# First attention of a small decoder on one core: normalisation in halves, a result's rest before maxima, copies behind exponentials

## The chip, the core and the metric

The kernel runs on one core of a Trainium2 chip. A core has five engines with an instruction stream each: TensorE (PE; its weight loads are shown apart as PEld), VectorE (DVE), ScalarE (ACT), GpSimd (POOL) and SyncE (SP). An engine takes its own stream in order, and the streams meet only at semaphores. The metric is device time in microseconds of one execution, smaller is better. The shown profile is one execution, with times counted from the first instruction of the program.

## The reference, cut to what matters

Two decoder layers over x of 16 sequences, 128 tokens and 256 features. The change touches the first sublayer alone, a 16-head attention with low-rank terms in its four weights:

```python
def _L0_attn_ref(x, Wq, bq, Bq, Aq, Wk, bk, Bk, Ak, Wv, bv, Bv, Av, Wo, bo, Bo, Ao):
    ...
    q = _split(lora_linear(x, Wq, bq, Bq, Aq))
    k = _split(lora_linear(x, Wk, bk, Bk, Ak))
    v = _split(lora_linear(x, Wv, bv, Bv, Av))
    scores = jnp.einsum('bhqd,bhkd->bhqk', q, k) * SCALE
    attn = jax.nn.softmax(scores, axis=-1)
    out = jnp.einsum('bhqk,bhkd->bhqd', attn, v)
    B, H, L, hd = out.shape
    out = out.transpose(0, 2, 1, 3).reshape(B, L, H * hd)
    return lora_linear(out, Wo, bo, Bo, Ao)
...
    x = x + _L0_attn_ref(_layernorm(x, axis=-1), ...)
    x = x + _L0_xattn_ref(ctx_2048, ctx_2048, _layernorm(x, axis=-1), L0_xattn_ssm_kernel, L0_xattn_D, 8)
    ...
```

## The kernel before, in words

The 16 sequences stay in on-chip memory as x, in four tiles of four. The attention (`stage_lora_attention`) has one loop of N = 64 steps n that each engine's block writes out in its own way: round g = n // 16 holds the four sequences of tile g, and step u = n % 16 of a round is one group of four heads of one sequence. The streams are written by hand; nothing schedules them. While round g computes its attention, the same loop prepares tile g + 1: its transposes, q, k and v.

What one group of heads n goes through, with the profile's lines: TensorE makes its scores in a bank (L343, for n + 4 and n + 5 in even steps); VectorE takes the negated maxima of each row (`row_max`, L589, for n + 3); ScalarE writes exponentials and row sums (`exps`, L520, for n + 2, four activations); VectorE inverts the sums (`inverse_sums`, L594, for n + 1); GpSimd multiplies the exponentials by them (`normalise`, L280, for n + 1); TensorE transposes the probabilities (`turn`, L353, for n); VectorE copies the transposed ones out (`keep_probT`, L599, for n); and TensorE multiplies them with the values (`weigh`, L365, for n - 1).

After four groups a sequence's result lies in one bank b_v. ScalarE takes its rounded half out (`keep_o`, L528), VectorE the rest (`o_rest`, L604), both in steps u = 1, 5, 9 and 13 for the sequence before; the next sequence's first `weigh` writes into the same bank and waits for that rest (`ot_lo`). `project` (L41 to L43) runs two steps later and `update` (L610) adds it to x.

The normalisation of a tile is VectorE's statistics (`vector_stats`, L112 to L119), a power on GpSimd (`pool_rstd`, L134), VectorE's application (`vector_apply`, L127), four transposes per half on TensorE (L139), and again a rounded half on ScalarE (`hi_chunk`, L146) and a rest on VectorE (`lo_chunk`, L150). Tiles 2 and 3 are normalised in rounds 0 and 1; the first tile of the next stage is in round 3. In round 2 VectorE adds a skip term instead (`add_skip`, L718), and GpSimd makes products for the next stage (L695) from step 31 on. In round 3 TensorE also runs convolutions for the next stage (L705 to L707), which ScalarE copies out (L713).

ScalarE copies q, k and v out of their banks in `keep_q` (L496, two activations), `keep_k` (L502) and `keep_v` (L512). TensorE makes these products at the end of steps 1, 5 (q), 3 with 7, 9 (k), 11, 13, 15 (v), each in bank b_p[0] or b_p[1], and waits for the copies before it uses the bank or the result again.

## Time and profile before

| what | value |
|---|---|
| time, median of 3 runs (all) | 1042.07 us (1040.94, 1042.07, 1046.86) |
| the profiled execution's own time | 1043.27 us |
| its span, first to last instruction | 1041.4 us |
| TensorE matmul busy | 968.2 us, 93% |
| VectorE, ScalarE, GpSimd busy | 61%, 47%, 23% |
| mean granted TensorE clock | 0.969 |
| first `turn` of the 64 steps, last one | 32.34 us, 195.84 us |

Busy shares are of the whole span, and the attention's 64 steps are under a sixth of it. A line of the timeline gives the start, the length, the engine, the line and the operation with its tiles; in brackets stands how long the engine was idle before it, and whose end released it. Matmuls overlap, so a matmul's busy time reaches over the start of the next one.

### The profile page before, as it was taken

The numbers are of one execution on the slowest core, as the hardware profiler recorded it, in microseconds if no ns is written. First come the engines' busy times: TensorE is split into PE (matmuls) and PEld (weight loads), VectorE is DVE, ScalarE is ACT, GpSimd is POOL, SyncE is SP. The second block draws the span as 40 slices with busy tenths as digits, with TensorE's granted clock in tenths as the row PEclk, the third lists the DMA queues.
The fourth block names the chain that finished last, engine by engine and source line by source line (L and its number), as shares of the span: only waits on it lengthen the run. The fifth ranks groups of instructions, "written<-read, shape, count | busy, mean of one in ns | idle before, by whom it ended". The sixth has DMA issues, their size and how long they took to land. (4 is left out here: it accounts for less than half of the span.)

```text
span 1041.4 us, 19631 instructions
## 1 busy us (share of the span) xinstructions
PE 968.2 (93%) x7397; PEld 827.0 (79%) x7397; DVE 639.3 (61%) x1399; ACT 484.8 (47%) x1611; POOL 238.3 (23%) x257
## 2 busy tenths in 40 slices
PE   7898989789989999999999999999999978899877
PEld 5676767689778888888888888888888857778757
DVE  5577777579757565654456644564464555777843
ACT  3577777533445454444444343444444433443421
POOL 3354677464002111111111111111111130110000
PEclk9899999989999999999999999999999998999969
DMA  7000000002240000000000000100000051000002
GB/s 298 2 2 2 2 2 2 25 1 82 82 162 2 1 1 1 2 1 2 1 1 2 1 1 2 41 1 1 1 1 1 1 177 83 2 1 1 3 1 81
DMA packets 10395, 27.85 MB, mean 27 GB/s; under 512 B 1792, under 2 KB 6944, under 8 KB 9664
## 3 DMA queue, kind: packets, MB, share of 16 engines
q1 hardware_dynamic: 9584, 26.41, 7.1%
q8 instruction: 60, 0.98, 0.4%
q10 hardware_dynamic: 720, 0.20, 0.1%
q14 instruction: 31, 0.25, 0.1%
HBM read 24.51 MB, written 2.10 MB: 26 GB/s over the span
## 5 line engine op out<-in xcount | busy, mean ns | idle before, releaser
L871 POOL TENSOR_TENSOR wa_prob<-wa_prob,wa_rsum 128x512 f32<-128x512 f32 x64 | 67.5, 1055 | 418.4 <-DVE wa_rsum L1409 418.4
L1213 ACT ACTIVATE wa_prob<-wa_prob,wa_negmax 128x128 f32<-128x128 f32 x256 | 99.8, 391 | 58.9 <-DVE wa_negmax L1398 58.7
L41 PE MATMUL bank<-norm_xT_hi,wide_hi 128*128 128x512 f32 x256 | 105.9, 414 | 2.2 <-DVE norm_xT_lo L150 1.4
L42 PE MATMUL bank<-norm_xT_lo,wide_hi 128*128 128x512 f32 x256 | 101.0, 395 | 0.0
L43 PE MATMUL bank<-norm_xT_hi,wide_lo 128*128 128x512 f32 x256 | 101.0, 395 | 0.0
L1465 DVE TENSOR_TENSOR wa_z_lo<-bank,wa_z_hi 128x512 fp32r<-128x512 f32 x64 | 44.3, 692 | 84.3 <-ACT wa_z_hi L1247 83.9
L520 ACT ACTIVATE v_prob<-bank,la_negmax 128x128 f32<-128x128 f32 x256 | 90.7, 386 | 1.2 <-DVE la_negmax L589 1.2
L1221 ACT COPY wa_q<-bank 128x512 f32<-128x512 f32 x64 | 37.6, 587 | 99.5 <-PE bank L43 99.5
L1228 ACT COPY wa_v<-bank 128x512 f32<-128x512 f32 x64 | 37.4, 585 | 97.5 <-PE bank L43 97.5
L280 POOL TENSOR_TENSOR v_prob<-v_prob,la_rsum 128x512 f32<-128x512 f32 x64 | 66.5, 1040 | 66.0 <-DVE la_rsum L594 65.9
L134 POOL TENSOR_TENSOR norm_rstd<-norm_rstd,minus_half 128x4 f32<-128x4 f32 x23 | 25.7, 1119 | 220.2 <-DVE norm_rstd L119 190.8
L41 PE MATMUL bank<-wide_hi,wa_z_hi 128*128 128x256 f32 x256 | 73.6, 287 | 1.7 <-DVE wa_z_lo L1465 1.4
L1404 DVE COPY wa_k<-bank 128x512 f32<-128x512 f32 x64 | 44.3, 692 | 50.3 <-PE bank L43 50.3
L1049 PEld LDWEIGHTS bank<-wa_probT,wa_v 128*128 128x128 f32 x512 | 65.4, 191 | 9.8 <-DVE wa_probT L1452 4.2
L43 PE MATMUL bank<-wide_hi,wa_z_lo 128*128 128x256 f32 x256 | 72.4, 283 | 0.0
L42 PE MATMUL bank<-wide_lo,wa_z_hi 128*128 128x256 f32 x256 | 72.3, 282 | 0.0
L1049 PE MATMUL bank<-wa_probT,wa_v 128*128 128x128 f32 x512 | 68.3, 276 | 1.9 <-DVE wa_probT L1452 1.9
L1452 DVE COPY wa_probT<-bank 128x512 f32<-128x512 f32 x64 | 44.1, 688 | 40.9 <-PE bank L1039 40.9
L998 PE MATMUL bank<-wa_k,wa_q 128*128 128x128 f32 x512 | 67.6, 275 | 0.0
L998 PEld LDWEIGHTS bank<-wa_k,wa_q 128*128 128x128 f32 x512 | 62.7, 192 | 0.4
L520 ACT ACTIVATION_READ_ACCUMULATOR v_prob<-bank,la_negmax 128x1 f32 x256 | 57.6, 225 | 0.0
L41 PEld LDWEIGHTS bank<-norm_xT_hi,wide_hi 128*128 128x128 f32 x256 | 48.2, 188 | 11.7 <-DVE norm_xT_lo L150 1.7
(273 smaller groups left out, 2473.0 us busy)
## 6 DMA issues: line engine op xcount, KB each, us to landing
wide_raw<-in_wide_w SPq DMA_DIRECT2D x16, 512.0 KB, 7.2
em_w<-in_em_w SPq DMA_DIRECT2D x1, 4096.0 KB, 15.0
x<-in_x SPq DMA_DIRECT2D x4, 512.0 KB, 4.9
lc_kt<-in_ctx_rev SPq DMA_DIRECT2D x1, 2048.0 KB, 10.3
lc_toep<-in_toeplitz SPq DMA_DIRECT2D x1, 2048.0 KB, 14.5
out_x<-x SPq DMA_DIRECT2D x8, 256.0 KB, 2.9
li_kt<-in_ctx_rev SPq DMA_DIRECT2D x1, 1536.0 KB, 7.3
w_or_y<-in_l_w SPq DMA_DIRECT2D x1, 1024.0 KB, 6.3
```

Source lines behind the costliest of these rows:

```text
L41: nc.tensor.matmul(out, a[0], b[0], start=start, stop=False, skip_group_check=True)
L42: nc.tensor.matmul(out, a[0], b[1], start=False, stop=False, skip_group_check=True)
L43: return nc.tensor.matmul(out, a[1], b[0], start=False, stop=stop, skip_group_check=True)
L280: nc.gpsimd.tensor_tensor(own, own, rsum[:, n % NS, :].unsqueeze(2).to_broadcast([P, 4, P]), ALU.mult)\
L520: last = nc.scalar.activation(prob[:, n % NP, s, :], b_s[n % RG][:, s * P:(s + 1) * P], ACT.Exp, bias=negmax[:, n % NS, s:s + 1], accum_ou ...
L871: nc.gpsimd.tensor_tensor(prob[:, s], prob[:, s], rsum[:, s, :].unsqueeze(2).to_broadcast([P, G, P]), ALU.mult).then_inc(prob_ok, 1)
L998: last = nc.tensor.matmul(b_s[s][:, t], q[:, s, t], k[:, s, t], start=True, stop=True)
L1049: last = nc.tensor.matmul(b_z[:, j * P:(j + 1) * P], v[:, g % 2, j, m * HD:(m + 1) * HD], probT[:, h_ % 2, j, :], start=True, stop=True)
L1213: last = nc.scalar.activation(prob[:, s, j, :], prob[:, s, j, :], ACT.Exp, bias=negmax[:, s, j:j + 1], scale=SCALE, accum_out=sums[:, s, j ...
L1404: nc.vector.tensor_copy(k[:, s, :], b_p[1][:, :]).then_inc(k_ok, 1)
L1452: nc.vector.tensor_copy(probT[:, t % 2], b_t[:, :].rearrange("p (j k) -> p j k", j=G))\
L1465: nc.vector.tensor_tensor(z[1][:, t % 2, :], b_z[:, :], z[0][:, t % 2, :].bitcast(F32), ALU.subtract).then_inc(z_lo, 1)
```

## The change

Three things move; no arithmetic changes. First, the statistics of a tile (four BN_STATS, then the aggregates) were all in step 3 of a round and the application in step 6. Now two BN_STATS are in step 3, two in step 5, the aggregates in step 6, GpSimd's power in step 6 instead of 3, and two applications each in steps 8 and 9. Second, `o_rest` comes before `row_max` (and `lo_chunk`) in its step. Third, `keep_q`, `keep_k` and the first `keep_v` of a tile come after the step's `exps` on ScalarE instead of before it (`extra_late`). Other stages still use the old functions.

```diff
--- before.py
+++ after.py
@@ -117,6 +117,31 @@
         chain.done(last)
         chain.close()
         nc.vector.tensor_scalar(self.rstd[:], self.meanvar[:, :, 1], EPS, None, ALU.add).then_inc(self.s_var, 1)
+
+    def vector_stats_half(self, dve, it, g, half):
+        for j in (2 * half, 2 * half + 1):
+            last = self.nc.vector.bn_stats(self.stats[:, j, :], self.pr.x[:, g * G + j, :])
+        if half == 1:
+            last.then_inc(self.s_chain, 1)
+
+    def vector_variance(self, dve, it):
+        nc = self.nc
+        dve.wait_ge(self.s_chain, 2 * (self.base + it) + 1)
+        nc.vector.memset(self.pr.wait_slot[:], 0.0)
+        for j in range(G):
+            last = nc.vector.bn_aggr(self.meanvar[:, j, :], self.stats[:, j, :])
+        last.then_inc(self.s_chain, 1)
+        dve.wait_ge(self.s_chain, 2 * (self.base + it) + 2)
+        nc.vector.tensor_scalar(self.rstd[:], self.meanvar[:, :, 1], EPS, None, ALU.add).then_inc(self.s_var, 1)
+
+    def vector_apply_half(self, dve, it, g, half):
+        if half == 0:
+            dve.wait_ge(self.s_pool, self.done(it))
+        for j in (2 * half, 2 * half + 1):
+            last = self.nc.vector.tensor_scalar(self.xn[:, j, :], self.pr.x[:, g * G + j, :], self.meanvar[:, j, 0:1],
+                                                self.rstd[:, j:j + 1], ALU.subtract, ALU.mult)
+        if half == 1:
+            last.then_inc(self.s_xn, 1)
 
     def vector_apply(self, dve, it, g=None):
         nc, x = self.nc, self.pr.x
@@ -228,8 +253,10 @@
 
 
 
-        STATS_AT, APPLY_AT, BIAS_AT = 3, 6, 10
+        STATS_AT, VAR_AT, POWER_AT, APPLY_AT, BIAS_AT = (3, 5), 6, 6, (8, 9), 10
         HI_AT, PROJECT_AT, ADD_AT = RG + 1, RG + 3, RG + 4
+
+        NORM_OF = {0: 2, 1: 3, NG - 1: NG}
 
         ORDER = (2, 0, 1, 3)
 
@@ -293,16 +320,14 @@
             for n in range(N - 1):
                 g, u = divmod(n, U)
                 normalise(n + 1)
-                if g + 2 < NG and u == STATS_AT:
-                    norm.pool_rstd(pool, g + 2)
+                if u == POWER_AT and g in NORM_OF:
+                    norm.pool_rstd(pool, NORM_OF[g])
                 if g + 1 < NG and BIAS_AT <= u < BIAS_AT + G:
                     add_bias(g + 1, u - BIAS_AT)
                 if FIRST <= n < FIRST + len(PIECES):
                     if n == FIRST:
                         pool.wait_ge(pr.conv_loaded, 16 * 4)
                     conv_piece(pr, *PIECES[n - FIRST]).then_inc(kk_first, 1)
-                if g == NG - 1 and u == STATS_AT:
-                    norm.pool_rstd(pool, NG)
 
         @block.tensor
         def _(pe):
@@ -536,7 +561,14 @@
                     return
                 if u == 1:
                     norm.hi_chunk(act, t, 1, b_p[0], xT[t % 2][0])
-                elif u == 2:
+                elif u == 11 and t + 1 < NG:
+                    norm.hi_chunk(act, t + 1, 0, b_p[0], xT[(t + 1) % 2][0])
+
+            def extra_late(g, u):
+                t = g + 1
+                if t == NG:
+                    return
+                if u == 2:
                     keep_q(t, 0, b_p[0])
                 elif u == 6:
                     keep_q(t, 1, b_p[1])
@@ -544,8 +576,6 @@
                     keep_k(t, 0, b_p[0])
                 elif u == 10:
                     keep_k(t, 1, b_p[0])
-                elif u == 11 and t + 1 < NG:
-                    norm.hi_chunk(act, t + 1, 0, b_p[0], xT[(t + 1) % 2][0])
                 elif u == 14:
                     keep_v(t, 0, b_p[1])
 
@@ -579,6 +609,8 @@
                     extra(g, u)
                 if n + 2 < N:
                     exps(n + 2)
+                if n < N:
+                    extra_late(g, u)
                 if N - U < n <= N:
                     keep_first_conv(n - (N - U) - 1)
 
@@ -610,19 +642,20 @@
                 nc.vector.tensor_tensor(x[:, b, :], b_p[1][:, 0:D], x[:, b, :], ALU.add).then_inc(x_ok, 1)
 
             def extra(g, u):
-                t = g + 1
-                if t + 1 < NG:
-                    if u == STATS_AT:
-                        dve.wait_ge(pr.x_loaded[t + 1], 16)
-                        norm.vector_stats(dve, t + 1)
-                    if u == APPLY_AT:
-                        norm.vector_apply(dve, t + 1)
-                if t == NG:
-                    if u == STATS_AT:
-                        dve.wait_ge(x_ok, G)
-                        norm.vector_stats(dve, NG)
-                    if u == APPLY_AT:
-                        norm.vector_apply(dve, NG)
+                it = NORM_OF.get(g)
+                if it is not None:
+                    own = it % NG
+                    if u == STATS_AT[0]:
+                        if it < NG:
+                            dve.wait_ge(pr.x_loaded[it], 16)
+                        else:
+                            dve.wait_ge(x_ok, G)
+                    if u in STATS_AT:
+                        norm.vector_stats_half(dve, it, own, STATS_AT.index(u))
+                    if u == VAR_AT:
+                        norm.vector_variance(dve, it)
+                    if u in APPLY_AT:
+                        norm.vector_apply_half(dve, it, own, APPLY_AT.index(u))
                 if g == 2:
                     if u == 0:
                         dve.wait_ge(pr.conv_loaded, 16 * 4)
@@ -658,15 +691,15 @@
                 g, u = divmod(n, U)
                 if n + 1 < N:
                     inverse_sums(n + 1)
+                b = batch_due(n, HI_AT)
+                if b is not None:
+                    o_rest(b)
                 if n + 3 < N:
                     row_max(n + 3)
                 if u == 1 and g + 1 < NG:
                     norm.lo_chunk(dve, g + 1, 1, b_p[0], *xT[(g + 1) % 2])
                 if u == 11 and g + 2 < NG:
                     norm.lo_chunk(dve, g + 2, 0, b_p[0], *xT[g % 2])
-                b = batch_due(n, HI_AT)
-                if b is not None:
-                    o_rest(b)
                 if n < N:
                     keep_probT(n)
                 b = batch_due(n, ADD_AT)
```

VectorE in steps 3 to 5 of a round; `norm_stats` are the statistics, `la_rsum` the inverted sums, `la_negmax` the maxima, `v_prob` the transposed probabilities. Before:

```order
L599 COPY v_prob<-bank 128x512
L112 BN_STATS norm_stats<-x 128x6 x4
L114 MEMSET wait_slot 1x1
L116 BN_AGGR norm_meanvar<-norm_stats 128x2 x4
L119 TENSOR_SCALAR norm_rstd<-norm_meanvar 128x4
L594 RECIPROCAL la_rsum<-la_sums 128x4
L589 TENSOR_REDUCE la_negmax<-bank 128x4
L599 COPY v_prob<-bank 128x512
L610 TENSOR_TENSOR x<-bank,x 128x256
L594 RECIPROCAL la_rsum<-la_sums 128x4
L589 TENSOR_REDUCE la_negmax<-bank 128x4
L604 TENSOR_TENSOR la_oT_lo<-bank,la_oT_hi 128x256
```

The same place of VectorE in the changed kernel:

```order
L631 COPY v_prob<-bank 128x512
L123 BN_STATS norm_stats<-x 128x6 x2
L626 RECIPROCAL la_rsum<-la_sums 128x4
L621 TENSOR_REDUCE la_negmax<-bank 128x4
L631 COPY v_prob<-bank 128x512
L642 TENSOR_TENSOR x<-bank,x 128x256
L626 RECIPROCAL la_rsum<-la_sums 128x4
L636 TENSOR_TENSOR la_oT_lo<-bank,la_oT_hi 128x256
L621 TENSOR_REDUCE la_negmax<-bank 128x4
L631 COPY v_prob<-bank 128x512
L123 BN_STATS norm_stats<-x 128x6 x2
```

Two BN_STATS instead of the whole group stand ahead of the first reciprocal, and in the second step the rest of the result stands ahead of the maxima.

ScalarE in steps 2 to 8 of a round; `la_q` and `la_k` are the copies, an `x4` of ACTIVATE is one group of heads. Before:

```order
L496 ACTIVATE la_q<-bank,la_q_bias,la_parity 128x512 x2
L520 ACTIVATE v_prob,la_sums<-bank,la_negmax 128x128 x12
L528 CAST la_oT_hi<-bank 128x256
L520 ACTIVATE v_prob,la_sums<-bank,la_negmax 128x128 x4
L496 ACTIVATE la_q<-bank,la_q_bias,la_parity 128x512 x2
L520 ACTIVATE v_prob,la_sums<-bank,la_negmax 128x128 x8
L502 ACTIVATE la_k<-bank,la_qk_bias 128x512
```

The same place of ScalarE in the changed kernel, from step 1 on:

```order
L545 ACTIVATE v_prob,la_sums<-bank,la_negmax 128x128 x8
L521 ACTIVATE la_q<-bank,la_q_bias,la_parity 128x512 x2
L545 ACTIVATE v_prob,la_sums<-bank,la_negmax 128x128 x8
L553 CAST la_oT_hi<-bank 128x256
L545 ACTIVATE v_prob,la_sums<-bank,la_negmax 128x128 x8
L521 ACTIVATE la_q<-bank,la_q_bias,la_parity 128x512 x2
```

Each copy has moved behind one group of exponentials.

## Rows read from the trace of the kernel before

**Rows 1.** Rounds 0, 1, 2: length; PE, PEld, DVE, ACT, POOL busy; granted clock; DMA.

```profile
32.34:75.83 43.49, 39.71 (x386) 29.88 (x386) 29.54 (x72) 30.17 (x142) 20.71 (x22) 0.90 0.01 2
...
75.83:117.21 41.38, 36.92 (x403) 28.11 (x401) 29.28 (x73) 30.64 (x144) 20.71 (x22) 1.00 0.01 2
...
117.21:158.33 41.12, 36.50 (x399) 27.62 (x397) 32.10 (x72) 29.99 (x143) 30.46 (x37) 1.00 0.01 2
```

**Rows 2.** Waits of TensorE's weighing, rounds 0 to 3: us, times, longest.

```profile
PE bank L365 <- DVE la_oT_lo L604: 1.2, 2, 0.7
...
PE bank L365 <- DVE la_oT_lo L604: 2.6, 3, 1.4
...
PE bank L365 <- DVE la_oT_lo L604: 4.6, 4, 1.4
...
PE bank L365 <- DVE la_oT_lo L604: 3.3, 4, 0.9
```

**Rows 3.** Waits of the transposes' weight loads, 28 to 204 us.

```profile
PEld bank L353 <- POOL v_prob L280: 8.1, 11, 2.1
```

**Rows 4.** Timeline, round 1, steps 2 to 5: start us, us, engine, line.

```profile
82.45 1.45 ACT L496 ACTIVATE la_q<-bank,la_q_bias,la_parity 128x512 f32<-128x512 f32 x2 [1.84 <-PE bank L43]
...
85.33 0.18 DVE L594 RECIPROCAL la_rsum<-la_sums 128x4 f32<-128x4 f32 x1 [1.75 <-ACT v_prob L520]
...
86.59 1.39 DVE L112 BATCH_NORM_STATS2 norm_stats<-x 128x6 f32<-128x256 f32 x4
...
86.79 0.42 PEld L353 LDWEIGHTS bank<-ident,v_prob 128*128 128x128 f32 x4 [0.39 <-POOL v_prob L280]
...
88.52 0.17 DVE L594 RECIPROCAL la_rsum<-la_sums 128x4 f32<-128x4 f32 x1
...
88.69 1.02 POOL L134 TENSOR_TENSOR norm_rstd<-norm_rstd,minus_half 128x4 f32<-128x4 f32 x1 [2.06 <-DVE norm_rstd L119]
...
90.77 0.66 PE L353 MATMUL bank<-ident,v_prob 128*128 128x128 f32 x4 [1.87 <-POOL v_prob L280]
```

**Rows 5.** Timeline, round 1, step 1.

```profile
78.05 0.41 ACT L528 CAST la_oT_hi<-bank 128x256 fp32r<-128x256 f32 x1
...
78.32 0.66 DVE L589 TENSOR_REDUCE la_negmax<-bank 128x4 f32<-128x512 f32 x1
...
79.22 0.69 DVE L150 TENSOR_TENSOR norm_xT_lo<-bank,norm_xT_hi 128x512 fp32r<-128x512 f32 x1 [0.24 <-ACT norm_xT_hi L146]
...
79.83 0.42 DVE L604 TENSOR_TENSOR la_oT_lo<-bank,la_oT_hi 128x256 fp32r<-128x256 f32 x1
...
80.39 0.43 PE L365 MATMUL bank<-v_prob 128*32 128x128 f32 x8 [1.39 <-DVE la_oT_lo L604]
```

**Rows 6.** Timeline, round 1, step 9.

```profile
99.92 0.37 ACT L528 CAST la_oT_hi<-bank 128x256 fp32r<-128x256 f32 x1
...
100.62 0.41 DVE L604 TENSOR_TENSOR la_oT_lo<-bank,la_oT_hi 128x256 fp32r<-128x256 f32 x1
...
101.19 0.43 PE L365 MATMUL bank<-v_prob 128*32 128x128 f32 x8 [0.74 <-DVE la_oT_lo L604]
```

**Rows 7.** Windows: step 5 of round 0, then step 5 of round 1.

```profile
47.94:51.66 3.72, 3.72 (x18) 2.55 (x19) 1.44 (x4) 0.04 (x1) 1.98 (x2) 0.54 0.00 0
...
90.77:92.97 2.20, 2.20 (x17) 1.62 (x18) 1.77 (x5) 0.04 (x1) 1.60 (x2) 1.00 0.00 0
```

**Rows 8.** Timeline, round 3, steps 9 and 10.

```profile
182.83 0.42 DVE L604 TENSOR_TENSOR la_oT_lo<-bank,la_oT_hi 128x256 fp32r<-128x256 f32 x1 [0.92 <-ACT la_oT_hi L528]
...
183.17 0.68 DVE L599 COPY v_prob<-bank 128x512 f32<-128x512 f32 x1
...
184.48 0.48 PEld L353 LDWEIGHTS bank<-ident,v_prob 128*128 128x128 f32 x4
```

**Rows 9.** One line's instructions, least, median and longest ns, rounds 0 to 3.

```profile
L718 DVE SCALAR_TENSOR_TENSOR lc_toep<-lc_anti,lc_skip,lc_toep x16: 341/574/1174, 118.9 to 157.6; 128x128 f32<-128x128 f32 x16
...
L127 DVE TENSOR_SCALAR norm_xn<-x,norm_meanvar,norm_rstd x12: 400/408/536, 53.1 to 176.2; 128x256 f32<-128x256 f32 x12
```

## Prediction

> **What bounds the kernel now.** I first read the windows over the rounds of the attention. In round 1 TensorE is busy for 36.92 of 41.38 us, VectorE for 29.28, ScalarE for 30.64 and GpSimd for 20.71; round 2 is alike, with VectorE at 32.10 of 41.12 [rows 1]. TensorE is the fullest engine by far, so its own idle time is what any reordering of the others can give back: about 4.5 us in each of the middle rounds, 11% of them. The reader is to see that no other engine is full: they matter by when they deliver, not by how much they do.
>
> Next I asked who TensorE waits for. Two things make up nearly all of it. `weigh` waits for `o_rest` 1.2 + 2.6 + 4.6 + 3.3 = 11.7 us, 13 times [rows 2]. And the weight loads of `turn` wait for `normalise` 8.1 us, 11 times, two of them over 2 us [rows 3]. Those last are mostly idle time of matmuls as well, but a short one hides under the last matmul's modelled end.
>
> Then the timeline says why. In round 1, ScalarE waits 1.84 us for the q product and copies it for 1.45 us, with the next exponentials behind it in its stream; VectorE's reciprocal for that group starts only at 85.33, 1.75 us idle; and `turn` of step 4 finds GpSimd 0.39 late at 86.79 [rows 4]. Right after, the statistics hold VectorE from 86.59 (four BN_STATS 1.39, then aggregates), so the reciprocal that `turn` of step 5 hangs on comes at 88.52; the power (1.02) stands ahead of its `normalise` on GpSimd; `turn` starts at 90.77 after 1.87 us of idle TensorE [rows 4]. In step 1, ScalarE had its half of the result at 78.05 + 0.41, but VectorE then did the maxima (0.66) and the xT rest, and only at 79.83 `o_rest`; `weigh` lost 1.39 us [rows 5].
>
> **The change, part by part.**
>
> *Statistics in halves, and copies behind the exponentials (one sum, since both make the same `turn` late).* The q copy's wait no longer stands before the exponentials of step 4: these need only their maxima and a free buffer, both there. So the reciprocal of `turn(4)` is limited by VectorE's own stream and the 0.39 goes. In step 3 two BN_STATS are left, 0.70 by half of 1.39. The reciprocal of `turn(5)` then stands behind 0.70 instead of 1.93 (86.59 to 88.52), and the power is not ahead of its product. TensorE's step 4 takes about 2.1 us (even steps without a wait: 2.20 in [rows 7]), more than reciprocal, `normalise` and their handovers together (86.79 to 88.9 against 0.17 + 1.04 + some 0.4), so `turn(5)` no longer waits. Of the 8.1 us in [rows 3] I leave 0.2 for each of five loads that have this gap with no wait at all, and 0.2 for the power, which in step 6 now stands ahead of the product for step 8: 8.1 - 1.0 - 0.2 = 6.9 us gained.
>
> Moved work costs: the second half of the statistics (0.70) is in step 5, aggregates and the added epsilon (some 0.5) in step 6, and two applications of 0.41 [rows 9] each in steps 8 and 9. They lie in VectorE's idle time (12.1 us in round 1, [rows 1]). Behind them stand one reciprocal each; for these the same 2.1 us of TensorE is the cover, and without it each would cost its own length, 0.5 to 0.8. The transposes of the new tile come in step 10, a step behind the last application, so nothing waits there. The waits inside the statistics are the old ones.
>
> The copies: q of step 2 now ends some 1.4 us behind its exponentials at worst. By this timeline the exponentials fit wholly into the 1.84 us in which ScalarE was idle, so q itself comes no later. The second k copy, wanted by the transposes at the end of step 10, has the least slack; I worked it through from step 1 with the rows' durations and find some 0.7 us left. Cost 0; without that cover up to 0.7 per round in three rounds, 2.1.
>
> *`o_rest` ahead of the maxima.* It cannot start before ScalarE's half. In step 9 of round 1 that half ends at 99.92 + 0.37 = 100.29, so `o_rest` could start near 100.33 instead of 100.62: `weigh`'s wait falls from 0.74 to 0.45 [rows 6]. So 0.45 is a floor: ScalarE's 0.37, VectorE's 0.41 and handovers, less the `turn` between. Thirteen waits at this floor are 5.9 us; 11.7 - 5.9 = 5.8 is the most that can go. Not all does. In step 1 of rounds 1 and 2 the next q product also needs the xT rest (0.69), which is pushed back behind `o_rest`, so of the gain of 0.94 there only about 0.4 stays, 1.1 lost on two. In round 3 `o_rest` already found VectorE idle, waiting 0.92 us for ScalarE [rows 8]; for three such steps, 1.0 us above the floor altogether, nothing changes. That leaves 5.8 - 1.1 - 1.0 = 3.7 us gained.
>
> *What comes back.* Steps 5 of rounds 0 and 1 have no `weigh` wait now because their `turn` is so late; once it is early they show the floor, 2 x 0.45 = +0.9. In round 3 the maxima (0.66) used to fill VectorE's wait for ScalarE; now they come after it, and push `keep_probT` from 183.17 to about 183.8. It ends at 184.5, and `turn` started at 184.48 [rows 8]: +0.2 on two steps, +0.4. In round 2 VectorE is fuller and `add_skip` takes 341 to 1174 ns [rows 9]; I allow +0.7 for round 2.
>
> *The clock.* Step 5 of round 0 ran at a granted clock of 0.54, 3.72 us against 2.20 for the same step of round 1 at 1.00 [rows 7]: the level of 1.2 GHz came right behind the step in which TensorE had idled. With that idle time gone I expect 2.4 GHz there: 1.5 us gained. The row that speaks against certainty: round 1 has the same idle time of 1.87 us [rows 4] and stayed at 1.00 [rows 1]. The Trainium skill ("TensorE: Matmul & The Clock Gate", What's actually happening) says that the half clock is the default, that activity releases it, and that the place of the switch depends on a phase the kernel does not set. By that rule the 1.5 may be absent or come back elsewhere, and the sum would be 1.5 less; the trace agrees, with its two equal gaps and one drop.
>
> *VectorE beside GpSimd.* `add_skip`, on two tensors, took from 341 to 1174 ns, while the twelve applications took 400 to 536 [rows 9]. I cost an application at its median of 0.41. The Trainium skill ("Perfetto Trace Analysis", Optimizing Scalar/DVE Operations) says that VectorE and GpSimd share a read port, which a two-port VectorE operation holds as an exclusive lock; it speaks against putting applications in two more steps beside GpSimd's products. By that rule an application could be as late as the longest `add_skip`, and the sum would be that of the second rival below.
>
> **Sum.** 6.9 + 3.7 + 1.5 - 0.9 - 0.4 - 0.7 = 10.1 us. From the profiled execution's own 1043.27 us that is 1033.2; from the median of 1042.07, 1.2 lower, 1032.0. Everything behind the attention is untouched. I take 1033.
>
> **Rivals.**
> *The clock does not repay (or dips elsewhere).* 10.1 - 1.5 = 8.6 gained: 1034 us (1034.7 from the profiled execution, 1033.5 from the median). For it: the two equal gaps above.
> *VectorE gives back half.* Its stream has 9 us of slack in a round 2 of 41 us [rows 1], 6.5 in one 2.3 shorter. If one application of each half waits for GpSimd's product and takes 1.17 like the longest `add_skip` instead of 0.54, a reciprocal or `o_rest` is 0.63 late at six places (3.8), and the second k copy behind them costs its 2.1: 10.1 - 5.9 = 4.2 gained, 1038.5 us, as the middle between the two starting points. For it: the 1174 ns. Against it: applications have been at 536 ns at the most.
> *It doesn't do what it says.* The wait for a result's rest is really ScalarE's, and the two long waits of `turn` (2.1 each, [rows 3]) come back at `weigh`. Then 10.1 - 3.7 - 4.2 = 2.2 is gained: 1040.5 us. For it: three places of round 3. Against it: [rows 5, 6] have VectorE busy with other work while the half lay ready.
> *Slower: VectorE stands before ScalarE's half with the maxima behind it.* There are 14 steps with both. A maximum can be late by 0.41 + 0.66 = 1.07 and more where ScalarE is late (0.92 idle before `o_rest`, [rows 8]). If all 14 reach the exponentials and so `turn`, that costs 15.0, and a TensorE that idles this often does not get its clock back either: 1042.07 + 15.0 - 8.6 = 1048.5 us. It takes the whole gain from 8.6 / 14 = 0.6 per step on. For it: an in-order stream behind a wait. Against it: maxima run one step ahead of their exponentials (n + 3 against n + 2), a step being 2.1 us or more.
>
> **Numbers.** The forecast 0.50, clock 0.17, half given back 0.18, nothing moved 0.10, slower 0.05. The range reaches from 1028 (neither the 1.1 and 1.0 lost nor the 0.4 and 0.7 given back, 13.3 gained from the median, and 0.8 for the runs' own spread) to 1040, which takes in the half given back and most of the third rival. A measurement of this kernel can tell about 0.5%, 5.2 us, from no change. The first two cases are faster, half of the third is too, a little of the others: faster 0.77, within 0.5% 0.18, slower 0.05.
>
> **What would show it.** In the changed kernel's profile: rounds 0 to 3 shorter by about 4.7, 2.9, 2.3 and 0.2 us (the terms above by their rounds); no wait of `turn` for `normalise` over 0.5 us after the first step; the waits of `weigh` for `o_rest` near 0.45 each, some 15 of them and 7 to 8 us in all; no idle ScalarE before L521 with exponentials behind it; the clock at 1.00 from step 2 on. Wrong would be: reciprocals late behind applications in steps 8 and 9; `row_max` late with ScalarE idle for it; TensorE waiting for a q or k copy; or the rounds shorter and the time behind 204 us longer.

## The result, and the profile after

The changed kernel takes 1031.84 us in the median of 5 runs (1030.38 to 1032.77), the kernel before beside it 1042.72 (5 runs, 1040.94 to 1046.86): a ratio of 0.9892, with an interval from 0.9872 to 0.9911. That is 10.9 us, inside the range of the prediction and 1.2 from its 1033. The profiled execution is one of the 1030.38 us, with a span of 1028.6 at a mean granted clock of 0.972.

The windows over the four rounds and over all of them; columns as in [rows 1]:

```profile
30.27:68.48 38.21, 36.81 (x386) 28.25 (x386) 29.32 (x72) 29.70 (x142) 21.07 (x22) 0.96 0.01 2
68.48:107.22 38.74, 36.65 (x403) 28.30 (x401) 29.19 (x72) 30.07 (x144) 21.26 (x23) 1.00 0.01 2
107.22:145.43 38.21, 36.11 (x399) 27.78 (x398) 30.81 (x73) 29.58 (x143) 30.02 (x37) 1.00 0.01 2
145.43:182.63 37.20, 34.08 (x381) 27.63 (x380) 25.54 (x64) 26.56 (x131) 26.32 (x31) 1.00 0.01 2
30.27:182.63 152.36, 143.66 (x1560) 111.95 (x1561) 114.86 (x280) 115.92 (x560) 98.68 (x110) 0.99 0.01 2
```

Busy times hardly moved: VectorE 29.19 us in round 1 after 29.28, ScalarE 30.07 after 30.64 [rows 1]. Round 1 is 2.64 us shorter, nearly all of it because TensorE idles 2.1 us in it instead of 4.5. The rounds are 5.29, 2.64, 2.91 and 0.31 us shorter, where 4.7, 2.9, 2.3 and 0.2 were forecast. They are 11.2 us together. The other 1.7 of the 12.9 between the two profiled executions lie where nothing was changed: the first round starts at 30.27 instead of 32.34, and what follows the rounds takes 0.4 longer. Over the fourteen kernels of this study that start lies anywhere from 30.27 to 32.54, and what follows the rounds takes 843.1 to 846.0 us. So I compare kernels by the length of the four rounds ("the loop"), less steps 0 to 2 of round 0, whose clock depends on what came before them: 154.46 us before, 144.31 after. A step runs from the first weight load of one `turn` to that of the next.

Whom TensorE waits for, 28 to 204 us: us, times, longest.

```profile
PE bank L390 <- DVE la_oT_lo L636: 7.2, 13, 0.9
...
PEld bank L378 <- issue: 6.8, 21, 2.8
...
PE bank L378 <- POOL v_prob L307: 2.6, 1, 2.6
```

The row of [rows 3], weight loads of `turn` (now L378) waiting for `normalise`, is not there any more. The one wait of `turn` for `normalise` that is left is that of the attention's very first group, 2.6 us, which the kernel before has too. `weigh` (L390) still waits for `o_rest` 13 times; nine of these are 0.45 or 0.46, one 0.48, three 0.88.

The timeline of round 1, steps 2 to 5, the place of [rows 4]:

```profile
74.49 1.49 ACT L521 ACTIVATE la_q<-bank,la_q_bias,la_parity 128x512 f32<-128x512 f32 x2
...
77.57 0.74 DVE L123 BATCH_NORM_STATS2 norm_stats<-x 128x6 f32<-128x256 f32 x2
78.23 0.16 DVE L626 RECIPROCAL la_rsum<-la_sums 128x4 f32<-128x4 f32 x1
78.47 1.04 POOL L307 TENSOR_TENSOR v_prob<-v_prob,la_rsum 128x512 f32<-128x512 f32 x1 [1.64 <-DVE la_rsum L626]
...
80.69 0.42 PEld L378 LDWEIGHTS bank<-ident,v_prob 128*128 128x128 f32 x4 [0.20 <-issue]
80.83 0.37 ACT L553 CAST la_oT_hi<-bank 128x256 fp32r<-128x256 f32 x1 [2.06 <-PE bank L390]
81.24 0.42 DVE L636 TENSOR_TENSOR la_oT_lo<-bank,la_oT_hi 128x256 fp32r<-128x256 f32 x1 [0.77 <-ACT la_oT_hi L553]
81.81 0.43 PE L390 MATMUL bank<-v_prob 128*32 128x128 f32 x8 [0.46 <-DVE la_oT_lo L636]
```

The q copy waits for nothing. Two BN_STATS (0.74) stand ahead of the reciprocal where four and the aggregates stood, and GpSimd multiplies at once: its product ends at 79.51, more than a microsecond before `turn` of step 5 loads. The price stands in the last three rows: ScalarE now sits idle until TensorE has finished a matmul, VectorE until ScalarE has taken the half, and TensorE in turn sits idle 0.46 us while the half (0.37) and the rest (0.42) are copied. With ScalarE and VectorE both idle ahead of their copies, no other order of VectorE can lower this floor.

### The profile page after: what moved, and what is told of

It is laid out like the page before. It is cut to its first block and busy times, and to the rows that moved or that the text cites. A ratio compares the mean times of both kernels' runs of the same rounds, so it can differ in the third digit from the quotient of the medians.

```text
span 1028.6 us, 19631 instructions
## 1 busy us (share of the span) xinstructions
PE 962.5 (94%) x7397; PEld 824.2 (80%) x7397; DVE 637.1 (62%) x1399; ACT 482.9 (47%) x1611; POOL 238.2 (23%) x257
```

## The experiments

Theory: the gain is the sum of TensorE's waits that the three parts take away, each part's own as the prediction's sum has them, and the clock of one step. Rivals: parts take away each other's waits; the clock is chance; what still stands is set by TensorE's own order. Edits are against the changed kernel. All times are medians beside the kernel before on the same chip (1041.85, 17 runs, for the three with one part and `whole_power6`; 1042.37, 11 runs, for the three with one part undone and `rest_late_round3`; 1042.24, 11 runs, for `half_before_conv`, `product_first`, `product_lo_first` and `all_first`), but for the changed kernel, whose 1031.84 stands beside 1042.72.

### One part alone

`stats_only`, the statistics in halves without the two other parts:

```diff
+                    extra_late(g, u)
                 if n + 2 < N:
                     exps(n + 2)
-                if n < N:
-                    extra_late(g, u)
...
-                b = batch_due(n, HI_AT)
-                if b is not None:
-                    o_rest(b)
                 if n + 3 < N:
                     row_max(n + 3)
...
+                b = batch_due(n, HI_AT)
+                if b is not None:
+                    o_rest(b)
```

> The kernel before with only the statistics and normalisation in halves (copies still ahead of the exponentials, the rest of a result behind the maxima). My theory: TensorE's transposes of step 5 in rounds 0 and 1 lose their 2 us waits, and the slow clock of that step in round 0 goes too, but the wait for the rest of a result shows itself there with over 1 us, as in round 2. About 3.5 us faster than before, 1039 us; rounds 0 and 1 shorter by 2 to 3 and by 1, rounds 2 and 3 by 0.3 or less. Rival (the gain is mostly the start ahead of the loop and its clock, by luck): rounds 1 to 3 as before, and no difference from before beyond 1 us.

`rest_only`, `o_rest` ahead of `row_max` alone; the first hunk above and this one:

```diff
-        STATS_AT, VAR_AT, POWER_AT, APPLY_AT, BIAS_AT = (3, 5), 6, 6, (8, 9), 10
+        STATS_AT, POWER_AT, APPLY_AT, BIAS_AT = 3, 3, 6, 10
...
-                    if u in STATS_AT:
-                        norm.vector_stats_half(dve, it, own, STATS_AT.index(u))
...
+                        norm.vector_stats(dve, it)
+                    if u == APPLY_AT:
+                        norm.vector_apply(dve, it)
```

> The kernel before with only the rest of a result ahead of the maxima. My theory: the thirteen waits of the weighing for the rest shrink toward 0.45 each, except in round 3 and where the next product waits for xT's rest; 3.5 us faster, 1039 us, of it 2.4 in round 2, and the two 2 us waits of the transposes in step 5 stay. Rival (the wait is ScalarE's own): the 13 waits keep their 11.7 us and the time is within 1 us of before.

`copies_only`, `extra_late` behind `exps` alone: the hunk of `rest_only`, and the second and third of `stats_only`.

> The kernel before with only the copies of q, k and v behind the exponentials. My theory: the 0.2 to 0.4 us waits of the transposes in steps 4 and 8 go, and because VectorE's copy of step 3 comes 1.5 us earlier the statistics do too, so that the 2 us waits in step 5 shrink to about 0.5 us. 4 us faster, 1038.5 us. Rival (the copies were covered and only the statistics' length matters): the waits in step 5 keep 1.5 us or more and the time is within 1.5 us of before.

| kernel | median us | ratio, interval | rounds 0 to 3 | loop less steps 0 to 2 |
|---|---|---|---|---|
| before | 1041.85 | 1 | 43.50 41.38 41.12 37.51 | 154.46 |
| stats_only | 1035.74 | 0.9932, 0.9914 to 0.9951 | 39.85 40.17 41.13 37.51 | 150.44 |
| rest_only | 1038.92 | 0.9978, 0.9962 to 0.9994 | 42.22 43.29 39.05 37.32 | 153.83 |
| copies_only | 1035.62 | 0.9939, 0.9915 to 0.9962 | 41.05 39.87 38.97 37.66 | 149.50 |
| after | 1031.84 | 0.9892, 0.9872 to 0.9911 | 38.21 38.74 38.21 37.20 | 144.31 |

By the loop the statistics give 4.0 us, the copies 5.0, the order 0.6; by the medians 6.1, 6.2 and 2.9. The largest difference is that of the order: its profiled execution lost 2.9 us to a clock dip in round 1 that the kernel before does not have (below). Without it the order alone would have given 3.5 in the loop. Expected of the medians were 3.5 for the statistics and for the order and 4 for the copies; the order came near it, the other two gave more.

In round 3 `rest_only`, `copies_only` and `no_stats` are not quite the kernel before: that one has GpSimd make its piece for the next stage ahead of the power, these have the piece between the power and the product that `turn` waits for. Timeline of `rest_only`:

```profile
166.37 1.02 POOL L159 TENSOR_TENSOR norm_rstd<-norm_rstd,minus_half 128x4 f32<-128x4 f32 x1 [2.84 <-DVE norm_rstd L119]
167.35 0.84 POOL L723 TENSOR_TENSOR lc_kk<-lc_kt 128x384 f32<-128x384 f32 x1
168.14 1.05 POOL L307 TENSOR_TENSOR v_prob<-v_prob,la_rsum 128x512 f32<-128x512 f32 x1
```

It costs them 0.80 to 0.82 us of wait of `turn` in step 5 of round 3, and 0.2 us of steps 4 and 5 against the kernel before, too little to change what follows.

The surprise is `copies_only`. Its round 2 fell from 41.12 to 38.97, though it has neither of the parts that were to help `weigh`. Its timeline in round 2, step 5:

```profile
125.36 0.66 DVE L621 TENSOR_REDUCE la_negmax<-bank 128x4 f32<-128x512 f32 x1
...
125.55 0.37 ACT L553 CAST la_oT_hi<-bank 128x256 fp32r<-128x256 f32 x1 [2.08 <-PE bank L390]
...
125.95 0.42 DVE L636 TENSOR_TENSOR la_oT_lo<-bank,la_oT_hi 128x256 fp32r<-128x256 f32 x1
...
126.52 0.43 PE L390 MATMUL bank<-v_prob 128*32 128x128 f32 x8 [0.46 <-DVE la_oT_lo L636]
```

The maxima still stand ahead of `o_rest`, but VectorE reaches them before the half is there, and the wait is at its floor all the same. Here VectorE no longer runs behind once the exponentials come early. But `rest_only` brings the same three waits to 0.65, 0.55 and 0.46, and its round 2 to 39.05: in round 2 either part takes the wait, and neither is its one cause. One expectation failed: with the copies alone the wait of `turn` in step 5 was to shrink to about 0.5 us, and it is 1.69 in round 0 and 0.98 in round 1.

### One part undone

`no_stats` has only the hunk that is shown under `rest_only`, `no_copies` the first hunk of `stats_only`, and `no_rest` its second and third.

> The changed kernel with the statistics and application back as before (all statistics and the power in step 3, application in step 6). My theory: transposes of step 5 in rounds 0 and 1 wait 1.2 us again, less the 0.45 of the rest's floor that this hides: 1.5 to 3 us slower than the changed kernel, 1033.5 to 1035 us (the upper end if the clock falls in round 0 again). Rival (with the copies moved, the statistics fit in idle time anyway): within 0.5 us of the changed kernel.

> The changed kernel with the rest of a result behind the maxima again. My theory: every wait of the weighing outside round 3 grows by 0.3 to 0.7 us over its floor, in the two steps 5 of rounds 0 and 1 too: 4 us slower than the changed kernel, 1036 us; round 3 not slower. Rival: the rest waits for ScalarE in any case, within 1 us of the changed kernel.

> The changed kernel with the copies of q, k and v ahead of the exponentials again. My theory: transposes of steps 4 and 8 in rounds 0 to 2 wait 0.2 to 0.4 us again, and the step behind may too: 2 us slower than the changed kernel, 1034 us, all of it in rounds 0 to 2. Rival (the copies are covered once the statistics are in halves): within 0.5 us of the changed kernel.

| kernel | median us | ratio, interval | loop less steps 0 to 2, against after |
|---|---|---|---|
| no_stats | 1033.43 | 0.9912, 0.9896 to 0.9928 | +3.47 |
| no_rest | 1032.16 | 0.9902, 0.9882 to 0.9921 | +2.31 |
| no_copies | 1033.85 | 0.9909, 0.9887 to 0.9931 | +1.86 |

By the loop the parts (statistics, order, copies) give 4.0, 0.6 and 5.0 us alone; taken away last they cost 3.5, 2.3 and 1.9. The medians of the last three are 1.6, 0.3 and 2.0 above the changed kernel's, and their intervals overlap with its own. The 3.5 holds a clock dip: three executions of `no_stats` took 1032.1 to 1032.2 us at a mean granted clock of 0.974 or 0.975, three 1034.7 to 1035.4 at 0.969 or 0.970, and the profiled one is of these. With all dips taken out at what they cost (1.5 or 1.6 in round 0, 2.9 in round 1; see below), the parts give 2.5, 3.5 and 5.0 alone, 11.0 in sum, all three at once give 8.6, and taken away last they cost 1.9, 2.3 and 1.9, 6.1 in sum. So much of a wait is taken away by either of two parts, and no part has a price of its own. The order of `o_rest` was expected to be worth about 4; by its median it can't be told from the change, and the trace gives it 2.3. TensorE's waits for `o_rest` there, us, times, longest:

```profile
PE bank L390 <- DVE la_oT_lo L636: 11.2, 15, 1.4
```

Five of the fifteen carry nearly all of the difference: 1.39 in step 1 of rounds 1 and 2, 0.89 in step 1 of round 3, and 0.81 in step 9 of rounds 0 and 1. Round 2 behind its step 1 is at 0.46, 0.46 and 0.54.

### The power, and the clock

`whole_power6` takes the statistics whole in step 3, but leaves the power and the halved application where the change has them:

```diff
-        STATS_AT, VAR_AT, POWER_AT, APPLY_AT, BIAS_AT = (3, 5), 6, 6, (8, 9), 10
+        STATS_AT, VAR_AT, POWER_AT, APPLY_AT, BIAS_AT = (3, 3), 3, 6, (8, 9), 10
...
-                        norm.vector_stats_half(dve, it, own, STATS_AT.index(u))
+                    if u == STATS_AT[0]:
+                        norm.vector_stats_half(dve, it, own, 0)
+                        norm.vector_stats_half(dve, it, own, 1)
```

> The changed kernel with all statistics back in step 3 in one piece, but GpSimd's power left in step 6 and the application in steps 8 and 9. It separates VectorE's time from the power that stood ahead of a product on GpSimd. My theory: recip of step 5 is 1.2 us later than in the changed kernel, but its product no longer waits 1 us for the power, so transposes of step 5 wait 0.3 us or less: within 1 us of the changed kernel, 1032 to 1033 us. Rival (the length of the statistics alone makes the wait): 1 us or more of wait in step 5 of rounds 0 and 1, 1034.5 us or more.

It took 1031.51 us (0.9897, 0.9878 to 0.9916), the loop 0.5 us more than after. The time came as expected; the wait of `turn` in step 5 was to be 0.3 or less and is 0.92 in round 0, 0.21 in round 1. The same `turn`, step 5 of round 0, in the timelines of `no_stats` and of `whole_power6`:

```profile
45.38 0.66 PE L378 MATMUL bank<-ident,v_prob 128*128 128x128 f32 x4 [1.68 <-POOL v_prob L307]
```

```profile
44.17 0.63 PE L378 MATMUL bank<-ident,v_prob 128*128 128x128 f32 x4 [0.92 <-DVE v_prob L631]
```

So the power (1.01) ahead of the product on GpSimd made 0.76 us of the 1.68, and in round 1, 0.98 against 0.21, 0.77. With the power gone, what is left ends with VectorE's `keep_probT` (L631), whose stream the whole statistics hold up. Moving the power, with the application in halves, brought 3.0 of the 3.5 us that `no_stats` lacks (1.6 of them its dip); the statistics in halves add 0.5. The power moved by itself was not run.

Five kernels (before, `rest_only`, `copies_only`, `no_stats`, `whole_power6`) have this stall of `turn` in step 5 of rounds 0 and 1, from 0.21 to 1.88 us long, and so show what follows it on the clock. Windows behind the stall, of `copies_only` (1.69 us of idle TensorE before it, round 0), of `rest_only` (1.88, round 1), and step 5 of round 0 of the changed kernel (none):

```profile
46.88:52.88 6.00, 6.00 (x51) 4.50 (x50) 3.77 (x11) 4.15 (x18) 1.97 (x2) 0.72 0.00 0
```

```profile
88.00:98.00 10.00, 10.00 (x71) 7.30 (x70) 5.64 (x14) 4.53 (x19) 3.86 (x4) 0.69 0.01 3
```

```profile
42.05:44.78 2.73, 2.27 (x22) 1.65 (x18) 2.19 (x5) 2.60 (x15) 0.78 (x1) 1.00 0.00 0
```

A mean of 0.72 or 0.69 is a stretch part at 2.4 and part at 1.2 GHz, with TensorE busy all the time. Of the six stalls of 1.68 to 1.88 us, five were followed by such a stretch (only the one of [rows 4] was not); of the four of 0.98 or less none, nor of the three of 0.80 to 0.82 in round 3. From step 3 of round 0 to the end of round 3 the fourteen kernels have no dip but these five. A dip cost from 1.5 us (the kernel before, steps 5 and 6 of round 0: 5.93 against 4.41 without a dip in the same steps of round 1) over 1.6 (`copies_only`, the same steps of round 0: 5.99) to 2.9 (`rest_only`, in round 1: 7.27). That last dip is also why `rest_only` shows 0.6 us and not 3.5; and of the 3.5 of `no_stats`, 1.6 are its dip in round 0.

### What is still paid in round 3

`rest_late_round3` undoes the order in round 3 alone, where the prediction saw a loss of 0.4:

```diff
-                if b is not None:
+                if b is not None and g < NG - 1:
                     o_rest(b)
                 if n + 3 < N:
                     row_max(n + 3)
+                if b is not None and g >= NG - 1:
+                    o_rest(b)
```

> The changed kernel with the rest of a result behind the maxima in round 3 alone, where VectorE had idled for ScalarE's half. My theory of the give-back: the copy of transposed probabilities is 0.66 us earlier there and round 3 is 0.2 to 0.4 us shorter but for step 1, where it loses 0.4: round 3 within 0.3 us of the changed kernel's 37.20, the time the same. Rival (the maxima behind the rest cost round 3 a full 0.66 in each of three steps): round 3 shorter by 1.5 us.

1031.29 us (0.9894, 0.9879 to 0.991): the same time. Round 3 is 37.52 us, 0.32 longer than after, by the wait of its step 1. The other steps differ by 0.1 or less either way, 0 in all: the order costs nothing in this round, and gives 0.3.

Three waits of 0.88 in round 3 are longer than the floor. The changed kernel's timeline has, in step 5:

```profile
158.13 0.40 ACT L746 COPY w_or_y<-bank 128x288 f32<-128x288 f32 x1 [0.96 <-PE bank L740]
158.42 0.38 ACT L553 CAST la_oT_hi<-bank 128x256 fp32r<-128x256 f32 x1
158.83 0.42 DVE L636 TENSOR_TENSOR la_oT_lo<-bank,la_oT_hi 128x256 fp32r<-128x256 f32 x1 [1.46 <-ACT la_oT_hi L553]
...
159.40 0.43 PE L390 MATMUL bank<-v_prob 128*32 128x128 f32 x8 [0.88 <-DVE la_oT_lo L636]
```

ScalarE's copy of a convolution result stands ahead of the half. `half_before_conv` has it behind:

```diff
-                if b is not None:
+                if b is not None and not N - U < n - 1 <= N:
                     keep_o(b)
...
                 if N - U < n <= N:
+                    b = batch_due(n + 1, HI_AT)
+                    if b is not None:
+                        keep_o(b)
                     keep_first_conv(n - (N - U) - 1)
```

> The changed kernel, but in round 3 ScalarE takes the half of a result before it copies out the convolution of the step before. My theory: the three waits of 0.88 us in steps 5, 9 and 13 of round 3 are the floor of 0.46 plus ScalarE's copy of the convolution ahead of the half: they fall to 0.46 to 0.5, round 3 from 37.20 to 36.0 us, the time 1 us shorter, 1030.8 us. Rival (they are VectorE's, maxima first): still 0.88.

1028.28 us (0.9862, 0.9845 to 0.988), the loop 2.2 us shorter, round 3 34.91 instead of 37.20. Its timeline at the same place:

```profile
159.54 0.37 ACT L553 CAST la_oT_hi<-bank 128x256 fp32r<-128x256 f32 x1
...
159.95 0.42 DVE L639 TENSOR_TENSOR la_oT_lo<-bank,la_oT_hi 128x256 fp32r<-128x256 f32 x1 [0.25 <-ACT la_oT_hi L553]
...
160.45 0.40 ACT L749 COPY w_or_y<-bank 128x288 f32<-128x288 f32 x1 [0.53 <-PE bank L743]
...
160.78 0.42 PE L390 MATMUL bank<-v_prob 128*32 128x128 f32 x8
```

Steps 5 and 9 fell from 2.76 to 1.72 us each: not the 0.42 above the floor but all of the wait (in step 13 it is 0.55). ScalarE's copy of step 4's convolution can only start when TensorE has made it, and the half stood behind that copy. Now the half (159.54) and the rest (159.95) are taken while TensorE makes this convolution, and both copies lie under it.

### TensorE's own order

If the floor is two copies with nothing of TensorE's over them, other TensorE work of the step put ahead of `weigh` must hide it. `product_first`:

```diff
-                if 1 <= n <= N:
+                waits_for_rest = n % RG == 1 and n > 1
+                if 1 <= n <= N and not waits_for_rest:
                     weigh(n - 1)
...
                     first_conv(n - (N - U) - 1)
+                if 1 <= n <= N and waits_for_rest:
+                    weigh(n - 1)
```

> The changed kernel, but in each step u = 1, 5, 9, 13 TensorE does the step's product for the next tile (or round 3's convolution) before the weighing that waits for the rest of a result. My theory: 0.46 us per wait is what ScalarE's half, VectorE's rest and their handovers cost over one set of transposes, and any TensorE work between hides it. Waits of the weighing gone in steps 5, 9, 13 of all rounds (14 us-tenths each in rounds 0 to 2, 0.9 each in round 3) and nothing gained in step 1 of rounds 1 and 2, where the product itself waits for xT's rest: the 64 steps shorter by 6 to 7 us, about 146 us from the first transposes to the last, and 1025 us. Rival (the later weighing makes later steps late: its bank, the half of the next result): under 2 us gained.

`product_lo_first` also has the xT rest of step 1 ahead of the maxima:

```diff
-                if n + 3 < N:
-                    row_max(n + 3)
                 if u == 1 and g + 1 < NG:
                     norm.lo_chunk(dve, g + 1, 1, b_p[0], *xT[(g + 1) % 2])
+                if n + 3 < N:
+                    row_max(n + 3)
```

> The kernel product_first and in addition VectorE writes xT's rest ahead of the maxima in step 1. My theory: the product's wait in step 1 of rounds 1 and 2 shrinks by the length of one row of maxima, 0.66 each: 1.3 us faster than product_first, 1024 us. Rival: the maxima are late and their exponentials with them, no gain over product_first.

`all_first` is `product_lo_first` and `half_before_conv` together:

> product_lo_first and half_before_conv together. With the convolution between transposes and weighing, the half is needed 0.8 us later, so the order on ScalarE should no longer matter: within 0.5 us of product_lo_first, 1024 us. Rival (waits add up): another 1.2 us faster than it.

| kernel | median us | ratio, interval | loop less steps 0 to 2 |
|---|---|---|---|
| product_first | 1025.45 | 0.9850, 0.9826 to 0.9873 | 139.65 |
| product_lo_first | 1025.03 | 0.9832, 0.9813 to 0.9851 | 139.25 |
| all_first | 1024.73 | 0.9825, 0.9803 to 0.9847 | 138.03 |

With `product_first` no wait of `weigh` for `o_rest` is left in rounds 0 to 3. Its windows, rounds 0 and 1:

```profile
31.83:68.34 36.51, 36.48 (x386) 27.95 (x387) 29.07 (x72) 29.56 (x142) 21.11 (x22) 0.95 0.01 2
68.34:105.89 37.55, 36.39 (x403) 27.81 (x402) 28.96 (x72) 30.15 (x144) 21.30 (x23) 1.00 0.01 2
```

The 1025 came as expected, but the loop is 4.7 us shorter than after where 6 to 7 were. In round 1 TensorE idles 1.16 us of 37.55, and that is one wait: step 1's q product for the xT rest, which now stands ahead of `weigh` and is no longer covered by it (step 1 is 3.81 us, 3.12 after):

```profile
71.93 0.68 DVE L175 TENSOR_TENSOR norm_xT_lo<-bank,norm_xT_hi 128x512 fp32r<-128x512 f32 x1
...
72.66 0.50 PE L41 MATMUL bank<-norm_xT_hi,la_w_hi 128*128 128x512 f32 x1 [1.16 <-DVE norm_xT_lo L175]
```

In round 3 a new wait comes: `turn` finds `keep_probT` late. So the round is only 0.57 us shorter than after. Over the rounds:

```profile
PE bank L378 <- DVE v_prob L634: 1.9, 3, 0.7
```

This is the wait that the prediction put at 0.2 a step in the changed kernel, where `weigh`'s own wait still hid it. `product_lo_first` was to take 0.66 from the step 1 of two rounds and took 0.2 each (1.16 to 0.96): with the maxima out of the way, ScalarE's half of xT is the next to be late. Its timeline in round 1:

```profile
72.55 0.69 DVE L175 TENSOR_TENSOR norm_xT_lo<-bank,norm_xT_hi 128x512 fp32r<-128x512 f32 x1 [0.31 <-ACT norm_xT_hi L171]
...
73.29 0.50 PE L41 MATMUL bank<-norm_xT_hi,la_w_hi 128*128 128x512 f32 x1 [0.96 <-DVE norm_xT_lo L175]
```

`all_first` has the lowest median, 7 us below the change's, though it can't be told from `product_lo_first` (0.3 apart). In the loop it is 1.2 us shorter, as its rival said and the theory did not: steps 5 and 9 of round 3 are 2.06 us instead of 2.76. Its rounds take 146.07 us, with TensorE busy for 143.12:

```profile
31.76:177.83 146.07, 143.12 (x1559) 110.67 (x1560) 115.05 (x280) 115.62 (x560) 98.61 (x110) 0.99 0.01 2
```

## Why the prediction was right, and where its terms were not

**Halves and copies, 6.9.** Steps 3, 4, 7 and 8 together lost 3.0 us in round 0, 2.3 in round 1, 0.5 in round 2 and 0.3 in round 3, 6.1 in all. The mechanism was the one told: the reciprocal is early, and `turn` waits for nothing. The term was 0.8 too large; I had allowed 0.2 a load for what hides under a matmul's modelled end. (The 2.20 us that the prediction takes from [rows 7] for an even step are of step 5, an odd one whose `weigh` did not wait; even steps without a wait take 2.20 as well, so nothing hangs on it. The slack of 6.5 us in the second rival should be 6.7.)

**`o_rest` ahead of the maxima, 3.7, and round 2's 0.7.** This step credited one part alone with what another takes as well. The steps of `weigh`, without the new floors, lost 3.4 us, where 3.7 - 0.4 - 0.7 = 2.6 was in the sum. But `copies_only` takes round 2's waits from 1.24, 1.15 and 0.78 us to 0.46, 0.46 and 0.60 with the order as it was, and the order taken away last costs 2.3, not 3.7. I had read "VectorE was busy with other work while the half lay ready" at two places of round 1 as a matter of order in all ten outside round 3's last three. In step 1 that was so: 0.6 us in each of two rounds, and the xT rest took back its part as told (a wait of 0.68 of the q product, in rounds 1 and 2). In round 2 VectorE was late with ScalarE, and earlier exponentials or the new order each suffice against it. The 0.7 held back for its fullness never came: the round lost 2.9 us, 2.3 forecast.

**The floors, 0.9.** They came, 0.53 us of step in step 5 of rounds 0 and 1, 1.06 together; the wait itself is 0.46 against an estimate of 0.45. In all `weigh` waits 7.2 us in 13 waits, where some 15 with 7 to 8 us were forecast.

**Round 3, 0.4.** The direct test shows 0 for it, and 0.3 gained in step 1. The late `keep_probT` is real, but lies under a longer wait; it shows as 0.59 to 0.67 us once that wait is gone. What round 3 did show is a wait in step 5 that grew from 0.62 to 0.88 us (the step by 0.41), behind a `turn` that is no longer late: the same exchange as the floors of rounds 0 and 1, at a place where I had not looked for it.

**The clock, 1.5.** Step 5 of round 0 went from 3.72 to 2.73 us: 1.5 less by the clock, 0.53 more by the floor. The size was exact. That it was the stall's doing and not luck is made likely by five of six long stalls with a dip, none of seven short ones, and no dip anywhere else in the rounds behind step 2; it is a likelihood, not a law, as round 1 of before shows. The rival that the clock does not repay is not borne out here. The 1.0 us that steps 0 to 2 of round 0 also lost was not predicted and is chance: `whole_power6`, with the same code there, has 9.05 us like the kernel before, the changed kernel 8.05. The Trainium skill ("TensorE: Matmul & The Clock Gate", What's actually happening) says that the place of the switch depends on a phase that the kernel does not set; for these steps the trace agrees.

**VectorE beside GpSimd.** Rival not borne out. The twelve applications in the changed kernel, least, median, longest:

```profile
L141 DVE TENSOR_SCALAR norm_xn<-x,norm_meanvar,norm_rstd x12: 402/406/758, 51.0 to 171.4; 128x256 f32<-128x256 f32 x12
```

One of twelve took 0.35 us longer, and nothing behind it was late. It is in round 3, and the only one of the twelve that had a GpSimd operation beside it:

```profile
167.31 0.74 POOL L728 TENSOR_TENSOR lc_kk<-lc_kt 128x256 f32<-128x256 f32 x1
167.44 1.08 DVE L141 TENSOR_SCALAR norm_xn<-x,norm_meanvar,norm_rstd 128x256 f32<-128x256 f32 x2
```

In the kernel before, too, the longest of the rounds' twelve (536 ns) was the only one with GpSimd beside it. The Trainium skill ("Perfetto Trace Analysis", Optimizing Scalar/DVE Operations) says that VectorE and GpSimd share a read port, which a two-port VectorE operation holds as an exclusive lock; the trace agrees with it in that one case each. So the rival stayed away because the two engines hardly met in steps 8 and 9, and not because meeting is free: the 536 ns that I held against it said as little.

**The sum.** 6.1 + 3.4 - 1.06 + 1.5 + 0.2 in small differences of round 3 is the 10.15 us of the loop less steps 0 to 2; the forecast was 10.1. That it was right to 0.1 is luck, since errors of both signs met: 0.8 too much at `turn`, 0.8 too little at `weigh`. The medians say 10.9 with an interval of about 2 us each way, and can't check single terms; the step lengths can.

What stays open: why one stall of 1.87 us was not followed by a dip, and why the start of the first round moves by 2 us between kernels that are the same up to there.

## What to carry to other kernels

Before you credit a wait to the order of the engine waited for, ask why that engine was late at all: if its stream merely runs behind, the work that frees it upstream takes the wait away without touching the order, and two such edits share one gain. When the late deliveries are gone, what is left of a wait is a chain of copies with too little over it, and independent work of the waiting engine has to lie over that chain. Where such work can be moved ahead of the wait, move it: here that gave 4.7 us more for a four-line edit. Where it is there already, let the chain start in time: in round 3 the half ahead of the convolution's copy gave 2.2 us. With both, and the xT rest ahead of the maxima, it was 6.3. Look at engines other than the bottleneck for one operation standing ahead of an urgent one: the power on GpSimd was 0.77 us of a stall, and the convolution's copy on ScalarE made those 2.2.

## What the runs showed of the hardware

- Idle TensorE of 1.68 to 1.88 us was followed by a stretch at the lower clock in five of six cases, one of 0.21 to 0.98 in none of seven; a dip cost 1.5 to 2.9 us, on top of stalls of 1.68 to 1.88.
- Handing a 128x256 result from TensorE through ScalarE's half (0.37) and VectorE's rest (0.42) leaves TensorE idle 0.46 us with one `turn` over it, alike at nine places of three rounds.
- Applications of 128x256 on VectorE took 402 to 409 ns with GpSimd idle; the one of the twelve beside a GpSimd operation took 758, and 536 in the kernel before.
- BN_STATS of 128x256 took 414 ns in the changed kernel's median, and 0.74 for two in a row.
- Between kernels whose code is the same at these places, the start of the first round moved by up to 2.3 us, and the 844 us behind the rounds by up to 2.9: single profiled executions can't be compared by their totals below that.
